# Expert weights loaded after the stores of the second normalisation, in 4 KB runs, with strided transposes in a graph and mixture-of-experts kernel

## What is computed

```python
x = x + gnn(layernorm(x), src, dst)        # h = nodes @ W + b; out[dst] = sum of alpha * h[src], softmax over in-edges
x = x + ffn(layernorm(x))                  # 8 experts, top 2, dense in the reference
# ffn: probs = softmax(xf @ Wg + bg); the two largest stay
for e in range(8):
    h = gelu(xf @ W1[e] + b1[e])           # W1[e]: 512 x 256
    y = h @ W2[e] + b2[e]                  # W2[e]: 256 x 512
    out = out + comb[:, e:e + 1] * y
```

## Time and profile before

| | us |
|---|---|
| median of 3 runs | 843.03 |
| lowest, highest | 835.05, 843.66 |
| the profiled execution | 843.71 |
| its span from first to last instruction | 842.0 |

### The profile page before, as it was taken

The page is one execution under the profiler, slowest core; times in us unless marked ns, Lnnn a source line. Parts: engine busy times, 40 slices in busy tenths (PEclk is TensorE's granted clock), DMA queues, the critical chain, the costliest instruction groups (busy, mean ns, idle before and its releaser), DMA issues.

```text
span 842.0 us, 14711 instructions
## 1 busy us (share of the span) xinstructions
PE 675.1 (80%) x3136; PEld 518.6 (62%) x3137; DVE 441.7 (52%) x1126; ACT 397.9 (47%) x1085; POOL 491.7 (58%) x610
## 2 busy tenths in 40 slices
PE   3999568979888888888888887497149999999960
PEld 2777457767776677777777776353046777766740
DVE  5899445555655555665565555691882222222220
ACT  4333255555555555555555555285103444444430
POOL 6000278877788787778778875101044677777750
PEclk9999879999999999999999999789569999999995
DMA  6243377777766767777777776199913677786767
GB/s 202 101 136 109 101 201 195 190 198 200 201 190 191 195 192 198 207 209 194 198 208 193 192 202 172 55 342 354 350 40 78 116 132 126 124 148 125 126 77 252
DMA packets 58538, 147.74 MB, mean 175 GB/s; under 512 B 8916, under 2 KB 18756, under 8 KB 58120
## 3 DMA queue, kind: packets, MB, share of 16 engines
q0 software_dynamic: 35456, 107.63, 51.9%
q1 hardware_dynamic: 22968, 37.16, 12.7%
q10 hardware_dynamic: 80, 2.56, 1.0%
HBM read 118.97 MB, written 33.47 MB: 181 GB/s over the span
## 4 chain that ended last, share of the span: by engine, by line
POOL 36%; PE 30%; issue 15%; DVE 10%; DMA 4%; ACT 1%; POOLq 1%; DVEq 0%; SPq 0%; ACTq 0%
POOL rows L488 32%; PE ps L808 9%; PE ps L818 9%; PE ps L644 4%; POOL idx L477 3%; PE ps L690 2%; PE ps L800 2%; PE ps L793 1%; DVE acc L1253 1%; DMA x_all<-in_x_dram 1%; DMA xn_table<-xn 1%; DVE junk L1071 1%; DMA rows<-node_table,idx 1%; PE ps L740 1%; DVE stats L1259 1%
## 5 line engine op out<-in xcount | busy, mean ns | idle before, releaser
L690 PE MATMUL ps<-rows,S 128*128 128x257 f32 x1568 | 365.9, 390 | 72.5 <-DVE S L1152 71.1
L690 PEld LDWEIGHTS ps<-rows,S 128*128 128x128 f32 x1568 | 298.2, 193 | 140.0 <-DVE S L1152 89.5
L488 POOL DMA_INDIRECT rows<-node_table,idx x316 | 313.7, 993 | 85.6 <-issue 74.8
L890 ACT ACTIVATE E<-sdst_b,rows 128x128 f32 x784 | 237.6, 388 | 191.4 <-DMA rows<-node_table,idx 191.3
L1146 DVE SCALAR_TENSOR_TENSOR Wt<-E 128x512 f32<-128x512 f32 x98 | 68.3, 696 | 140.6 <-ACT E L890 127.9
L1152 DVE SCALAR_TENSOR_TENSOR S<-node_id,dstT,Wt 128x128 f32<-128x128 f32 x392 | 112.1, 347 | 23.9 <-DVE Wt L1146 23.9
L808 PE MATMUL ps<-W_e,xgT 128*128 x352 | 85.0, 385 | 0.0
L818 PE MATMUL ps<-W_e,hidT 128*128 x176 | 82.8, 593 | 0.6 <-ACT hidT L987 0.6
L1159 DVE TENSOR_TENSOR acc<-acc,ps 128x514 f32 x99 | 67.9, 686 | 28.7 <-PE ps L690 20.2
L587 POOL DMA_INDIRECT result<-y,si x44 | 70.6, 1605 | 17.8 <-POOL gi L535 10.9
L477 POOL COPY idx<-srcT 128x4 int32 (+1 forms) x79 | 24.0, 303 | 84.1 <-DMA node_table<-rows 83.6
(11 more groups left out here) (192 smaller groups left out, 496.0 us busy)
## 6 DMA issues: line engine op xcount, KB each, us to landing
W_e<-in_L_ffn_W_dram SPq DMA_DIRECT2D x16, 512.0 KB, 6.4
node_table<-rows SPq DMA_DIRECT2D x20, 258.0 KB, 2.7
result<-acc SPq DMA_DIRECT2D x20, 256.0 KB, 5.0
xn_table<-xn SPq DMA_DIRECT2D x20, 256.0 KB, 5.3
rows<-node_table,idx POOLq DMA_INDIRECT x316, 3.7
x_all<-in_x_dram SPq DMA_DIRECT2D x19, 256.0 KB, 3.1
out_dram<-result SPq DMA_DIRECT2D x1, 2500.0 KB, 16.8
out_dram<-result ACTq DMA_DIRECT2D x1, 2500.0 KB, 18.4
```

Of the source, the lines that this page charges most:

```text
L488: nc.gpsimd.indirect_dma_start(out=rows[:, r, c, :], out_offset=None, in_=table, in_offset=bass.IndirectOffsetOnAxis(ap=idx[:, r, c:c + 1] ...
L690: m = pe.matmul(ps_agg[q][:, a, 0:HALF], S[:, w, c, :], rows[:, r, c, a * HALF:(a + 1) * HALF], start=(c == 0), stop=(c == GC - 1))
L890: m = nc.scalar.activation(e[:, q, c, :], sdst_b[:, bass.ds(tile * P, P)], ACT.Exp, bias=bias, scale=scale)
```

## The change

There are two parts.

- On SP the eight loads of W1 leave the loop of store steps and stand in a loop of their own behind all ten steps, ahead of the loads of W2.
- Partition p now holds the rows p*KT + k of W1 (p*HF + k of W2), k = 0 to 3 (0 to 1). These rows are neighbours in DRAM, so a partition's share of a matrix is one run of 4 KB. The contraction index of the products is thereby dealt out differently, and the transposes follow: block k of `xg` takes every fourth column (k, k + 4, ...), block k of `act_h` every second. Products, weights in SBUF and all sizes are the same.

```diff
             def load_W1(e):
 
-                sp.dma_start(W1_e[:, bass.ds(e, 1), :, :].rearrange("p e k f -> p (e k) f"),
-                             W1.rearrange("e (k p) f -> p e k f", p=P)[:, bass.ds(e, 1)]
-                             .rearrange("p e k f -> p (e k) f")).then_inc(ld_W1, 16)
+                sp.dma_start(W1_e[:, bass.ds(e, 1), :, :].rearrange("p e k f -> p (e k f)"),
+                             W1.rearrange("e (p k) f -> p e k f", p=P)[:, bass.ds(e, 1)]
+                             .rearrange("p e k f -> p (e k f)")).then_inc(ld_W1, 16)
 
             def load_W2(e):
 
-                sp.dma_start(W2_e[:, bass.ds(e, 1), :, :].rearrange("p e k d -> p (e k) d"),
-                             W2.rearrange("e (k p) d -> p e k d", p=P)[:, bass.ds(e, 1)]
-                             .rearrange("p e k d -> p (e k) d")).then_inc(ld_W2, 16)
+                sp.dma_start(W2_e[:, bass.ds(e, 1), :, :].rearrange("p e k d -> p (e k d)"),
+                             W2.rearrange("e (p k) d -> p e k d", p=P)[:, bass.ds(e, 1)]
+                             .rearrange("p e k d -> p (e k d)")).then_inc(ld_W2, 16)
...
             with sp.Fori(0, NX // 2) as i:
                 for s in range(2):
                     x_step(2 * i + s, s)
-                    load_W1(2 * i + s)
             for u in range(NX, NT // 2):
                 x_step(u, u % 2)
+            with sp.Fori(0, NX) as e:
+                load_W1(e)
             with sp.Fori(0, NX) as e:
                 load_W2(e)
...
                     for k in range(HF):
-                        m = pe.transpose(ps_hT[:, k * P:(k + 1) * P], act_h[:, s, k * P:(k + 1) * P], ident[:, :])
+                        m = pe.transpose(ps_hT[:, k * P:(k + 1) * P],
+                                         act_h[:, s, :].rearrange("p (f k) -> p f k", k=HF)[:, :, k], ident[:, :])
...
                     for k in range(KT):
-                        m = pe.transpose(ps_x[:, k * P:(k + 1) * P], xg[:, r, k * P:(k + 1) * P], ident[:, :])
+                        m = pe.transpose(ps_x[:, k * P:(k + 1) * P],
+                                         xg[:, r, :].rearrange("p (d k) -> p d k", k=KT)[:, :, k], ident[:, :])
```

## The result

| | before | after |
|---|---|---|
| median, 20 runs each (us) | 842.25 | 835.8 |
| lowest, highest | 834.21, 848.0 | 828.17, 843.65 |
| the profiled execution | 843.71 | 835.69 |
| its span | 842.0 | 834.0 |

The ratio after to before is 0.992, with a 95% interval of 0.9893 to 0.9947: 4.5 to 9.0 us shorter. The forecast was 846.5, that is 0.4% longer than before. The time lies inside the range and where the first rival stood (836.0), but the kernel moved the other way than forecast.

The account below looks back on a forecast made before the run. Waits for `xn` stores were taken to bound the second normalisation, PE the expert tiles. The forecast was 843.7 - 7.7 (store waits) + 10.5 (strided transposes) = 846.5 us, own range 841 to 853, whole range 834 to 860.

Parts of the forecast that it names:

- first rival: Strided loads in the expert tiles cost nothing, so only the 7.7 us gain counts: 836.0 us; chance 0.31.
- The W1 loads and the stores: Second normalisation: without W1 loads among them, stores cause no queue, pairs keep 3.38 us, and 7.7 us are gained.
- POOL's four stores, the lower bound: Second normalisation: if the last `xn` waits for all of POOL's 1.05 MB, 2.9 us, the gain is only 4.8 us.
- The late loads: Weights and biases, 11.5 MB behind the last store, arrive at 609 to 612, 9 to 12 us before the tiles need them.
- the second sum: Late weight and bias transfers at the lower rate of 364 GB/s take 31.6 us and end at 612.
- Runs of 4 KB: Weight transfers of 580 to 609: longer runs could move their end by 3 us either way; nothing waits, so zero.
- The strided transposes: Expert tiles: strided loads for 176 `xg` transposes cost 4.6 to 16.4 us, taken as 10.5 us.
- I take the middle, 60 ns and 10.5 us: Expert tiles: 60 ns more per `xg` transpose, chosen between 26 and 93 ns, adds 10.5 us.
- The extra of a load: Expert tiles: DVE's strided reads, 0.70 to 0.88 ns an element, imply 90 to 113 ns more per strided PE load.
- the room in the pace of the transposes: Expert tiles: 20 to 64 ns of each 110 ns transpose are free to hide a longer load.
- The low-clock reading of the earlier trace: First stage 3 loads, at 1.2 GHz, take up to 231 ns, 90 more; so only 20 of 110 ns are free.
- Nothing for `act_h`: Expert tiles: the 88 `act_h` loads at 8 bytes were given no cost, with ends of 0 and 8.2 us.

Follow-up runs that it names:

- e1: Kernel before with only the W1 loads moved behind all store steps, no strides or 4 KB runs; ratio to before 0.9863, second normalisation 38.7 us.
- e8: Kernel before with only the W1 loads moved behind all store steps, repeated on another chip; ratio to before 0.9874, second normalisation 38.3 us.
- e4: Kernel before with a W2 load beside the W1 load in each of the first eight store steps; ratio to before 1.0124, second normalisation 55.0 us.
- e9: Kernel before with four W1 loads behind the first four store steps, the other four behind all steps; second normalisation 40.5 us against 46.1 before.
- e10: Kernel before with four W1 loads behind store steps 4 to 7, the other four behind all steps; second normalisation 44.5 us against 46.1 before.
- e3: Changed kernel with 72 transposes added at PE's end, loading columns 4 to 64 bytes apart; median load 141 ns at 4 bytes, 209 at 8 and 16.
- e6: Changed kernel with transposes and short f32 products added at PE's end; from 4 to 16 bytes apart, transpose pace 109 to 120 ns, product pace 109 to 233.
- e7: Changed kernel run again, on the chip with the longer edge stage; ratio to before 0.9922, second normalisation 38.3 us, tile 4.16 us.
- e2: Changed kernel with the W1 loads back in the store loop, so strides and 4 KB runs alone; ratio to before 1.0004, second normalisation 46.4 us.
- e5: Changed kernel with a tile's four `xg` transposes reading f32 64 bytes apart in `xn2` instead of 16 bytes apart; tile 4.13 us.

## Why the prediction was wrong

The sum was 843.7 - 7.7 + 10.5.

- **The W1 loads and the stores: right in size, and in the cause but for one part.** Forecast 7.7 us, measured 7.5 in the stage (46.1 to 38.6; 46.1 to 38.7 with the order alone). PE runs at 3.38 to 3.39 us a pair to the end, as the step said. That bytes ahead of the stores are the cause was shown by e1 and e8 (none, 0.2 us of waits or less) and e4 (twice, twice the wait); e9 and e10 (same bytes, other place) favour a backlog. The prediction booked all of it as waits for stores; 1.9 us of it were PE at the low clock behind its longest wait. The sum came out because the start of the last pair before, 584.18, already had that in it. POOL's four stores, the lower bound, cost nothing that can be seen: ACT's only wait for a store was 0.2 us.
- **The late loads: right.** They were expected at 609 to 612 (the second sum, 579.2 + 31.6, makes 611) with the first copy at 613.7. In the profiled execution, which was 4 us early, they ended at 605.4 with the copy at 609.91.
- **Runs of 4 KB: right that they count nothing.** They end the transfers 2 us sooner, beside the routing (e1 against after).
- **The strided transposes: wrong, and this term alone turned the sign.** The step that failed is "I take the middle, 60 ns and 10.5 us". Measured, a transpose of `xg` in a tile takes 12 ns more (0.49 less 0.44 us over four). Both inputs were off on the same side. The extra of a load, carried over from DVE's rows as 90 to 113 ns, is 70 at 16 bytes (211 less 141). And the room in the pace of the transposes, put between 20 and 64 ns, is near its upper end: 70 of extra raise the pace by 11 (109 to 120), so 59 do not show. The low-clock reading of the earlier trace rows, from which the 20 came, gave no measure of it. In a tile that is 0.05 us in place of 0.24, and over the tiles 174.2 less 171.8 = 2.4 us in place of 10.5. With 2.4 the sum would have been 838.4, below the kernel before.
- **The first rival, 836.0: near, in part by luck.** Strided loads cost 2.4 us and not nothing. That the median fell on its number needs 2.5 us more of gain than the stages show (below).
- **Nothing for `act_h`: wrong in kind, right in size.** Its loads at 8 bytes pay nearly the same (195 ns), and the two transposes take 0.23 us in place of 0.22, 0.4 us in all. The Trainium skill, "SBUF — State Buffer", section "Door 1: The DMA port swizzle", asks for at least two accesses to a line of 16 bytes for full bandwidth, which loads at 8 bytes have. PE's loads here do not agree that this is enough: in e3 and e6 loads at 8 and at 16 bytes last the same, 209 ns. Nor does its "4 fp32" for free hold as read literally: the load at 16 bytes is 70 ns longer. That little of it reaches the time is put down here to the streamed identity, which no run shows by itself.

Index copy to output grew by 3.3 us (201.8 to 205.1), of which the strides are 2.4. Most of the rest is the clock at the first tiles: from the first `xg` transposes to the second of `act_h` it was 10.89 us before, 11.86 after and 11.71 with the order alone (e1), but 10.95 in e7. The first `xg` transposes of the profiled execution after ran at the low granted clock, 0.54 in 610 to 625, and took 1.13 us where they had taken 0.66. As e7 has the same strides and not this loss, and e1 has it without the strides, it is not a cost of the strides.

**What stays open.** By the stage lengths the change is worth 7.5 - 3.3 = 4.2 us, 0.5%; the measured 0.8% (0.5 to 1.1) just reaches that. e1 and e2 too came out shorter against before than their stages say: e1 11.6 us shorter where they say 6.6, e2 0.3 us longer where they say 2.9; e4 fits (10.5 against 9.7). The difference would lie in the edge stage ahead of the change, or in the one profile of the kernel before, if its stage was shorter than that of most executions. No instruction of the edge stage is changed, but its end scatters: PE's first transposes of stage 3 came at 544.5 before and at 540.5, 544.3, 539.6, 548.5 and 546.9 us in after and e1 to e4, without a pattern. One profile a kernel cannot tell scatter from a small effect. And no run varies the streamed length of a transpose alone, which would show what hides its strided load.

## What to carry to other kernels

Loads that nobody waits for yet belong behind the stores that an engine does wait for, as soon as both together want more than the DMA engines move; where they must stand among them, early ones cost less than late ones (about 2 us against 6 in e9 and e10, one execution each). Reckon a wait of PE by more than its idle time: what followed a wait of 3.2 us here ran at the low clock and lost 1.9 us more. A longer load of the stationary operand is not a longer transpose: measure how much of it reaches the pace at the operation itself, before it decides the sign. If a layout for long DMA runs makes the kernel read with a stride, ask first whether anything waits for those transfers; here the longer runs gained nothing and the strides cost 2.4 us.

## What the runs showed of the hardware that was not expected

A PE load of 128 f32 for a transpose takes 141 ns from neighbouring columns and mostly 191 to 211 ns at any distance from 8 to 64 bytes (e3, e6, e5, after). In a long row of transposes there is no difference between 8 and 16 bytes (209 and 209) and slightly less at 64 (196); of the two loads of `act_h` in a tile the median was 195. Beside a streamed identity of 128 columns the pace goes from 109 to 120 ns at 8 and 16 bytes and 113 at 64. A load for a plain f32 product with 8 streamed columns goes from a pace of 109 ns to 182 at 8 bytes, 233 at 16 and about 217 at 64, so there the distance costs up to 124 ns a pass.

After 3.2 us of idle time in the middle of the second normalisation (before) and 3.4 us (e10), the granted clock of PE fell (0.69 in 580 to 585; 0.55 in 648.5 to 654), and the same transposes and products took 1.9 and 2.5 us longer. No such fall followed single waits of 0.74 us (before, 1.00 in 570 to 575) and 0.86 us (e9, 1.00 in 635.6 to 640); in e2 one did follow several waits of 0.5 to 1.0 us close together (0.59 in 578.3 to 582.5).
